# Two column tiles of 64 nodes for the one-hot message products of a graph layer

## The reference

```python
h = silu(edge_lengths_embedding @ fc_w1 / sqrt(NB))          # NB = 8, 64 hidden
w = (h @ fc_w2 / sqrt(NH)).reshape(-1, NPATH, MUL)           # 5 paths of MUL = 64
s = node_features[:, :MUL][sender]
v = node_features[:, MUL:].reshape(-1, MUL, 3)[sender]
dot = einsum('eui,ei->eu', v, sh1); crs = cross(v, sh1[:, None, :])
m0 = (w[:, 0] * s + w[:, 3] * dot * inv_sqrt3) * inv_sqrt2
m1 = (w[:, 1] * s * sh1 + w[:, 2] * v + w[:, 4] * crs * inv_sqrt2) * inv_sqrt3
agg = segment_sum([m0, m1], receiver, 2500) / AVG_NEIGH
out = agg @ lin_w / sqrt(MUL)                                # lin_w0 for m0, lin_w1 for m1
x = layernorm(x + out + x)
```

## Time and profile before

| | us |
|---|---|
| median of three runs | 2748.4 (2746.8 to 2750.7) |
| span of the profiled execution | 2736.8 |
| tables | to 41 |
| messages | 41 to 1134 |
| order | 1134 to 1159 |
| projection | 1159 to 1364 |
| attention and output | 1364 to 2737 |

### The profile page before, as it was taken

One profiled execution on the slowest core, in us unless ns is written; L12 is line 12 of the kernel. 1 busy time (PEld: TensorE's weight loads), 2 busy tenths in 40 slices (PEclk: granted clock), 3 DMA queues, 4 the chain that ended last, 5 costly groups with the idle time before them and its releaser, 6 DMA issues. The chain is left out here.

```text
span 2736.8 us, 41806 instructions
## 1 busy us (share of the span) xinstructions
PE 2107.6 (77%) x9647; PEld 1611.0 (59%) x9647; DVE 2183.1 (80%) x3415; ACT 1524.3 (56%) x4291; POOL 1618.3 (59%) x1808
## 2 busy tenths in 40 slices
PE   3999999999999999679815666666566666656666
PEld 2787878777777777533314455455455545545555
DVE  6888888888888888645546878878888788878793
ACT  5787888788877887433223444444444444444443
POOL 5666666666666666342246666666666666666642
PEclk8999999999999999889957788878878878887787
DMA  6232222222222222769856666666666666666651
GB/s 203 72 84 81 83 83 83 83 82 84 83 83 81 84 82 84 167 165 253 234 181 168 168 173 175 173 165 173 177 169 175 169 172 176 167 175 170 173 141 45
DMA packets 157414, 379.08 MB, mean 139 GB/s; under 512 B 47810, under 2 KB 63298, under 8 KB 157186
## 3 DMA queue, kind: packets, MB, share of 16 engines
q0 software_dynamic: 100544, 309.00, 40.6%
q1 hardware_dynamic: 44946, 68.53, 8.7%
q10 hardware_dynamic: 11904, 1.34, 0.4%
HBM read 353.36 MB, written 37.07 MB: 143 GB/s over the span
## 5 line engine op out<-in xcount | busy, mean ns | idle before, releaser
L1358 POOL DMA_INDIRECT kv_e<-kv_rows,edge x752 | 716.9, 953 | 408.4 <-issue 223.4
L487 POOL DMA_INDIRECT feat<-in_x_rows,idx x664 | 677.1, 1020 | 236.2 <-issue 234.8
L523 ACT ACTIVATE vsh<-feat,rec_a 128x256 f32<-128x256 f32 x1980 | 806.8, 495 | 8.9 <-DMA feat<-in_x_rows,idx 4.8
L1541 PE MATMUL ps_sum<-kv_e,ident 128*128 128x264 f32 x1504 | 473.8, 477 | 376.9 <-issue 264.2
L1541 PEld LDWEIGHTS ps_sum<-kv_e,ident 128*128 128x128 f32 x1504 | 352.5, 240 | 481.8 <-issue 283.6
L571 PE MATMUL ps_a<-msg,hot 128*128 128x257 f32 x1312 | 409.4, 393 | 4.0 <-issue 4.0
L573 PE MATMUL ps_a<-msg,hot 128*128 128x256 f32 x1312 | 390.6, 379 | 0.1
L575 PE MATMUL ps_a<-msg,hot 128*128 128x192 f32 x1312 | 320.2, 325 | 0.0
L573 PEld LDWEIGHTS ps_a<-msg,hot 128*128 128x128 f32 x1312 | 248.6, 190 | 38.2 <-issue 1.9
L575 PEld LDWEIGHTS ps_a<-msg,hot 128*128 128x128 f32 x1312 | 248.8, 190 | 34.9
L571 PEld LDWEIGHTS ps_a<-msg,hot 128*128 128x128 f32 x1312 | 222.2, 189 | 66.3 <-issue 66.3
(11 more groups left out here) (419 smaller groups left out, 3182.2 us busy)
## 6 DMA issues: line engine op xcount, KB each, us to landing
ef<-in_ef_t SPq DMA_DIRECT2D x84, 256.0 KB
kv_e<-kv_rows,edge POOLq DMA_INDIRECT x752
rows_e<-rows SPq DMA_DIRECT2D x41, 272.0 KB
feat<-in_x_rows,idx POOLq DMA_INDIRECT x664
rows_e<-in_ef_t SPq DMA_DIRECT2D x1, 7446.0 KB, 26.6
kv_rows<-kv SPq DMA_DIRECT2D x20, 260.0 KB, 2.5
rows_e<-in_ef_t SPq DMA_DIRECT2D x1, 3706.0 KB
x<-x_rows SPq DMA_DIRECT2D x23, 128.0 KB
```

The lines of the kernel that those rows point to most:

```text
L487: pool.indirect_dma_start(out=feat[:, u, c, 0, :, :].rearrange("p a b -> p (a b)"), out_offset=None, in_=g.x_rows, in_offset=bass.Indirect ...
L523: ins = act.activation(vsh[:, u % TURN, c, j, :, :], feat[:, u % TURN, c, 0, :, :], ACT.Copy, scale=rec_a[:, u % 2, c, 1 + j:2 + j])
L1358: pool.indirect_dma_start(out=kv[:, u, s, :], out_offset=None, in_=g.kv_rows, in_offset=bass.IndirectOffsetOnAxis(ap=edge[:, u, s, DH + 1: ...
L1541: mm = pe.matmul(out, g.ident[:], kv[:, u, s, D:], start=(s == 0), stop=False, skip_group_check=True)
```

## The change

A step's range is now 64 nodes that begin at a multiple of 32, and the one-hot of a chunk has 64 columns. Chunks 0 and 2 are added in partitions 0 to 63 of `ps_a`, chunks 1 and 3 in partitions 64 to 127, so the matmuls of two chunks stand in two column tiles, written in turn. `sums` has 82 slabs instead of 43, one for each multiple of 32. In the projection a window of 128 nodes is reached by five slabs: ScalarE copies all five in one instruction, and TensorE multiplies each with one of five 0/1 matrices `place`, which put the 64 nodes of either side at their place in the window. The degrees in `stage_order` come from the same five matrices.

Memory is made by dropping two iotas, by halving the buffers of `vsh` (ScalarE waits two steps later in the count of products: m_prod against i + 3 instead of i + 1) and `emb`, by a shorter `msg`, and by putting work tensors of the tables into `feat`. The one-hot is made by adding the range's first node, taken from a table `origin`, to 0..63, and comparing.

```diff
 def one_hots(dve, g, out, sc, w):
-    nodes = g.iota_node[:, bass.ds(w * (P // 2), P)].rearrange("p (a n) -> p a n", a=1).broadcast_to([P, CHUNKS, P])
-    receivers = g.rec[:, bass.ds(sc * CHUNKS, CHUNKS), 0:1].broadcast_to([P, CHUNKS, P])
-    return dve.tensor_tensor(out, nodes, receivers, ALU.is_equal)
+    nodes = g.count512[:, 0:REACH].rearrange("p (a n) -> p a n", a=1).broadcast_to([P, CHUNKS, REACH])
+    receivers = g.rec[:, bass.ds(sc * CHUNKS, CHUNKS), 0:1].broadcast_to([P, CHUNKS, REACH])
+    return dve.scalar_tensor_tensor(out, nodes, g.origin[:, bass.ds(w, 1)], receivers, ALU.add, ALU.is_equal)
...
-            act.activation(g.sums[:], zero[:].rearrange("p (a b) -> p a b", a=1).broadcast_to([P, HALVES + 3, D + 1]),
+            act.activation(g.sums[:], zero[:].rearrange("p (a b) -> p a b", a=1).broadcast_to([P, SLABS, D + 1]),
...
-            dve.memset(g.codes[:], IDLE)
+            dve.memset(g.codes[:, 0:LAG], IDLE)
...
+            for k in range(PARTS + 1):
+                dve.tensor_scalar(g.place[:, k, :], g.count512[:, 0:P], spot[:, k:k + 1], None, ALU.is_equal)
...
-        emb = sb("emb", [P, 2, SUPER // 2])
+        emb = sb("emb", [P, SUPER // 2])
...
-        vsh = sb("vsh", [P, TURN, CHUNKS, 3, 4, MUL])
-        hot = sb("hot", [P, 2, CHUNKS, P])
-        msg = sb("msg", [P, 2, CHUNKS, 3 * D + 1])
+        vsh = sb("vsh", [P, 2, CHUNKS, 3, 4, MUL])
+        hot = sb("hot", [P, 2, CHUNKS, REACH])
+        msg = sb("msg", [P, 2, CHUNKS, 11 * MUL + 1])
...
-                act.wait_ge(m_prod, i + 1)
+                act.wait_ge(m_prod, i + TURN - 1)
...
-                    out = ps_a[:, u % 2, :]
-                    for c in range(CHUNKS):
-                        rows = msg[:, u % 2, c]
-                        pe.matmul(out[:, 0:D + 1], hot[:, u % 2, c, :], rows[:, 2 * D:3 * D + 1], start=(c == 0),
-                                  stop=False, skip_group_check=True)
-                        pe.matmul(out[:, 0:D], hot[:, u % 2, c, :], rows[:, D:2 * D], start=False, stop=False,
-                                  skip_group_check=True)
-                        mm = pe.matmul(out[:, MUL:D], hot[:, u % 2, c, :], rows[:, MUL:D], start=False,
-                                       stop=(c == CHUNKS - 1), skip_group_check=True)
+                    for c in range(0, CHUNKS, 2):
+                        for part, (at, lo, hi) in enumerate(((0, 7 * MUL, 11 * MUL + 1), (0, 3 * MUL, 7 * MUL), (MUL, 0, 3 * MUL))):
+                            first, last = c == 0 and part == 0, c == CHUNKS - 2 and part == 2
+                            for side in range(2):
+                                out = ps_a[side * REACH:(side + 1) * REACH, u % 2, at:at + hi - lo]
+                                mm = pe.matmul(out, hot[:, u % 2, c + side, :], msg[:, u % 2, c + side, lo:hi], start=first,
+                                               stop=last, skip_group_check=True)
...
-                act.activation(agg[:], g.sums[:, bass.ds(w * 2 + 1, 1), 0:D].rearrange("p a d -> p (a d)"), ACT.Copy)
-                act.activation(beside[0:half, :], g.sums[0:half, bass.ds(w * 2 + 2, 1), 0:D].rearrange("p a d -> p (a d)"),
-                               ACT.Copy)
-                act.activation(beside[half:, :], g.sums[half:, bass.ds(w * 2, 1), 0:D].rearrange("p a d -> p (a d)"),
-                               ACT.Copy).then_inc(p_agg, 1)
+                act.activation(agg[:], g.sums[:, bass.ds(w * PARTS, PARTS + 1), 0:D], ACT.Copy).then_inc(p_agg, 1)
...
-                    pe.matmul(ps_a[:, cols], agg[:, cols], g.ident[:], start=True, stop=False, skip_group_check=True)
-                    mm = pe.matmul(ps_a[:, cols], beside[:, cols], g.swap[:], start=False, stop=True, skip_group_check=True)
+                    for n in range(PARTS + 1):
+                        mm = pe.matmul(ps_a[:, cols], agg[:, n, cols], g.place[:, n, :], start=(n == 0), stop=(n == PARTS),
+                                       skip_group_check=True)
```

More of the change, by code:

```diff
@@ L543, in hidden_pair @@
                     rows = slice(step * NH, (step + 1) * NH)
-                    pe.matmul(ps_h[:, step, 0:SUPER // 2], g.w1[rows, :], emb[rows, u // 2 % 2, :], start=True, stop=True,
+                    pe.matmul(ps_h[:, step, 0:SUPER // 2], g.w1[rows, :], emb[rows, :], start=True, stop=True,
                               skip_group_check=True).then_inc(m_hps, 1)
@@ L725, in _ @@
         def _(pe):
-            pe.wait_ge(r_prior, 2)
-            pe.matmul(ps_p[:, 32:32 + WINDOWS], g.swap[:], beside[:], start=True, stop=True).then_inc(r_first, 1)
+            for k in range(PARTS + 1):
+                mm = pe.matmul(ps_p[:, 32:32 + WINDOWS], g.place[:, k, :],
+                               g.sums[:, k:k + PARTS * (WINDOWS - 1) + 1:PARTS, D], start=(k == 0), stop=(k == PARTS))
+            mm.then_inc(r_first, 1)
             pe.wait_ge(r_bins, 2)
```

167 lines of the change are left out of this document (89 added, 78 removed).

## The result

The changed kernel takes 3004.4 us (median of runs from 2961.0 to 3053.0) against 2747.6 before beside it: a ratio of 1.077, 95% interval 1.072 to 1.082. Times in this document are medians of all runs, ratios compare the faster runs alone (here 2961.0 and 2966.7, beside two of 3042.1 and 3053.0). The prediction was 2700, the range up to 2785.

| us | before | after | difference |
|---|---|---|---|
| first to last one-hot product of the message stage (start to start) | 1076.5 | 1278.6 | +202.1 |
| from there to the projection | 25.4 | 27.5 | +2.1 |
| projection and the start of attention, to its first gather of rows | 242.0 | 260.3 | +18.3 |
| all else | 1392.9 | 1392.9 | 0.0 |

A forecast was written before the change was run, and what follows sets the result against it. TensorE was taken to bound the message stage, then a chain over two steps. From 2748.4 us: -82 chain, -2 last products, +19 clock falls, +19 projection, -46 in all, 2702, rounded to 2700; range 2670 to 2785.

The forecast's parts named there:

- The chain: Message stage: dependent work through several engines over two steps, 12.03 us, becomes the bound in place of TensorE's 13.06; -82 us.
- the clock: Message stage: TensorE's idling lowers its clock, 1.6 us a fall; half of two in seven pairs taken, +19 us.
- the clock falls in most pairs: Rival, message stage: 1.6 us for each pair with a fall, half of the pairs 2748, all 2812; chance 0.10.
- no faster product moves it: Message stage: once products shrink by 0.52 of 4.72 us a step, the two-step chain binds, whatever the products take.
- something not seen: The remaining case beside the named ones, with no mechanism or time given; chance 0.02.
- Column tiles overlap: Message products in two column tiles overlap fully, 4.72 us a step becoming 2.36, pairs of passes 0.21 us apart.
- the shared-stream rival: Message products: two column tiles share one stream of reads and gain nothing, products 4.80 us a step, kernel 2780; chance 0.28.
- VectorE's wait moved to vsh: Message stage sign: VectorE waits no longer for the products before L101's successor, but before the first cross product for vsh.
- Half the vsh buffers: Message stage: ScalarE waits for the products of step i-2 instead of i-4; claimed to cost nothing.
- The time that GpSimd needs for the gathers: Rival, message stage: another engine binds first, gathers at 6.3 us a step instead of 6.02, kernel 2727; chance 0.05.
- The projection: Ten matmuls a window replace four, lasting 2.2 us, and the wait for ef goes; +19 us, between 14 and 29.
- The tables: Clearing sums grows from 9.4 to 17.9 us, hidden in ScalarE's 10.6 us of idle time; zero, up to +3.

The follow-up runs named there:

- x2: The changed kernel without the message stage's gathers, a constant 0.5 standing for the senders' features: 2762.9 us, ratio 1.000 to the kernel before.
- g4: The changed kernel with three small GpSimd copies as a pause ahead of each step's four gathers: 2538.1 us, ratio 1.006, before at 2523.2.
- b4: The kernel before with three small GpSimd copies (0.6 us) ahead of every run of gathers: 2528.5 us, ratio 1.003, before at 2524.3.
- g5: The changed kernel with the pause ahead of the gathers and the hidden pair ahead of TensorE's wait for messages: 2408.4 us, ratio 0.955.
- g2b: The changed kernel gathering 64 instead of 256 numbers a row, on a chip with before at 2749.0: 3062.3 us, ratio 1.111.
- x1: The changed kernel computing with zeros, its path weights scaled by 0 so all messages are zero: 3203.5 us, ratio 1.166.
- e3: The changed kernel with all products in one column tile, so they don't overlap: 3050.9 us in one run, beside before at 2931.2.
- e2: The kernel before with part of its message products left out, full array, no column tiles: 2809.3 us in one run, beside before at 2931.2.
- c1: The changed kernel again, unaltered, as a control: 3215.7 us, ratio 1.156, beside before at 2763.4.
- g2: The changed kernel gathering 64 instead of 256 numbers a row, on a chip with before at 2523.2: 2540.1 us, ratio 1.007.
- g4b: The changed kernel with the pause ahead of each step's gathers, on a chip with before at 2749.0: 3196.9 us, ratio 1.163.
- g5b: The changed kernel with the pause and the hidden pair ahead of the wait, on a chip with before at 2749.0: 2860.3 us, ratio 1.037.

## Why the prediction was wrong, and where it was right

**The size of the miss.** The prediction gave the message stage -84 + 19 = -65; it measured +202, a miss of 267. The chain alone, 12.03 us for each of 81.5 pairs, makes 980 us. Falls at 1.58 (x2's longest pair less the chain) in every pair, the most they can be, make 1109, and 1278.6 were measured: the falls take at most 129, and the rest, at least 169, goes to the pairs with holds. The working started from 13.06 a pair where the stage before averaged 13.21, its first pair being held 8.5 us (its products of 57.2 to 62.5 are reported at 69.19): it put the chain's gain 12 us too low, which lessened the miss. So 129 - 19 + 169 - 12 = 267.

**The step that failed first: the clock.** The price was right, 1.6 us a fall against 1.56 in the rows. The count was not. I took two in seven from the earlier trace rows and halved it, 12 falls; nearly every pair of after pays one, and 0.6 of x2's. The argument against it, that TensorE is busy 5 us between two gaps, rested on no row of the clock. And I had worked out two gaps, 1.2 and 2.7 us; once the clock has fallen, the slower even step fills the first (786.58 follows without idle time) and the odd step leaves all of it in one piece, 3.7 to 3.8 us (780.67, 794.27). A fall makes the next gap longer, which the gaps of 2.5 us in the earlier trace rows couldn't show, and of those two in seven fell already. The rival "the clock falls in most pairs" had it right in mechanism and in price, and got 0.10. It is what g4 shows: the change with a pause gives next to nothing in the messages there (1071 us from first to last product, where b4 has 1073), and costs 0.6% in all.
The Trainium skill, "TensorE: Matmul & The Clock Gate", Part 1, "HAM oscillation — how this bites in real kernels", describes kernels whose short bursts of matmuls are separated by waits and that start every burst at the low clock. The trace agrees, with slow weights in 73 of 82 pairs, 2.50 us long in most; there the waits are for DMAs, here for VectorE.

**The step that was missing: where the products end.** I treated the end of the products as free once it was early ("no faster product moves it"). This holds for the chain, and x2 confirms it: with the gathers gone, its shortest pairs take 12.02 us. It left out that TensorE's updates could be late at all, and that this hangs on what else runs when they fall due. Nothing in the rows ahead of the prediction shows such a wait. The trace of before does, in two places that I passed over: the first pair of the messages, at 57 to 69 us, and the attention stage, where GpSimd waits 96.4 us "remote". The "something not seen" had 0.02.

**What was right.** The chain of two steps. Column tiles overlap: 2.60 us for 24 passes, a pair of passes each 0.21; the shared-stream rival, 0.28, falls with it, and the step of L1035's moving operand stays as the likely cause of its slower pairs (not tested apart). VectorE's wait moved to vsh where holds leave it be: in x2 79.3 us before L634 and 43.2 before L106. It did not vanish before L106; the steps with the low clock end their products later. Half the vsh buffers cost nothing that shows: x2 has them, and reaches the chain's 12.03. The time that GpSimd needs for the gathers did not bind. The projection: +18.3 for +19. The ten matmuls take 2.50 us where I said 2.2, and the wait for ef is gone. After (timeline, waits):

```profile
1430.56 2.50 PE L1030 MATMUL ps_a<-place,agg 128*128 128x128 f32 x20
```

```profile
PE ps_e L1046 <- DMA ef<-in_ef_t: 0.2, 1, 0.2
```

The tables: 17.76 us for the clearing (17.9 predicted), and ScalarE still idles ahead of its next stage, as in the earlier trace rows:

```profile
16.45 17.76 ACT L264 ACTIVATE sums<-zero_t 128x21074 f32<-128x21074 f32 x1
...
42.05 0.21 ACT L534 ACTIVATE rec_a<-rec 128x16 f32 x1 [5.15 <-issue]
```

Even with no fall and no hold, the change as it stands was worth 65 us by this working (84 - 19), 2.4%, or 78 by the measured terms (1076.5 - 980 - 18), 2.8%: the next chain bounds the gain, and a fifth of it goes to the projection.

## What to carry to other kernels

When the bound engine gets shorter work, price the time it then idles: on TensorE a gap of 3.7 us in every 13.6 cost 1.6 us of each pair, and moving other matmuls into the gap, and off the chain, turned the change, on a chip without holds, from +0.6% (g4) into -4.5% (g5). Then look where the end of the shortened work falls among the other engines' bursts, since a completion can be delayed by them: leave the gathers out once, and the difference between x2 and the kernel as it is measures it. Run an unchanged control beside every experiment, since chips differ by more than the change does.

## What the runs showed of the hardware

- **Held updates.** On chips where most runs of the kernel before take 2741 to 2766 us, and on one where its only run took 2931, semaphore updates of finished matmuls came up to 9.8 us late in the trace after (11.6 in g2b) while GpSimd issued indirect DMAs one every 1.26 us. Three quarters of the late ones came 1.5 to 2.7 us after the start of the last gather of a run, queued ones 43 ns apart; once some 50 passes stood unreported in the rows shown (24, 8 and 19), pairs of passes started only every 1.4 us. Neither the values (x1), nor the bytes (g2b), nor idle time or a low clock (e3), nor column tiles (e2) are needed; the gathers are (x2). What within the chip delays the updates is open. So is whether SyncE's plain loads do it too, whether the message stage of the kernel before can be made to hold by shifting its gathers (b4), and whether recording a trace has a part in it, since every time here comes from an execution with a trace. The kernel before itself may be held more at times: on the chip of c1 three of its 13 runs took 2811.9, 2867.5 and 3009.3 us, and none of them left a trace to read.
- **Two kinds of chips.** On the two where before takes 2523 and 2524 us there was no hold in any of six kernels, and the same edits had holds on another chip (g2, g4 and g5 against g2b, g4b and g5b). From its first gather of rows to the end, which no edit touches, a kernel takes 1129 to 1132 us there instead of 1336 to 1361. That part too consists of gathers and TensorE's work, and updates in it are late on the slower chips (76 of 159 in before) and not on the faster ones (0 of 188 in g4). That all of the 205 us are holds was not tested.
- **A gather's cadence does not depend on its bytes**: four of them 1.26 us apart with full and with quarter rows.
- **The clock** kept 0.99 with gaps of 1.1 and 1.9 us in each pair of steps (g5), and fell in 73 of 82 pairs of after, where the gap is mostly 3.7 us or more. The gap alone doesn't decide it: in x2 gaps of 2.5 to 2.8 us stand before slow weights 13 times and before fast ones 13 times.
